# Four chained layers on one core: the attentions' exponentials go through one set of score banks, with bfloat16 row maxima

## What is computed

```python
scores = jnp.einsum('bshd,bmhd->bhsm', qh, kh) / jnp.sqrt(hd)   # layer 3: masked columns get -1e9
probs  = jax.nn.softmax(scores, axis=-1)                        # over the 77 context rows
out    = jnp.einsum('bhsm,bmhd->bshd', probs, vh)               # then a 256x256 projection and the residual
```

## Time and profile before

| | |
|---|---|
| median of 3 runs | 912.06 us |
| the profiled execution | 911.81 us |
| its span, first to last instruction | 909.6 us |
| PE, DVE and ACT busy | 92%, 57%, 49% of the span |
| mean granted TensorE clock | 0.977 of full speed |

### The profile page before, as it was taken

The page is one execution under the profiler, slowest core; times in us unless marked ns, Lnnn a source line. Parts: engine busy times, 40 slices in busy tenths (PEclk is TensorE's granted clock), DMA queues, the critical chain, the costliest instruction groups (busy, mean ns, idle before and its releaser), DMA issues.

```text
span 909.6 us, 10241 instructions
## 1 busy us (share of the span) xinstructions
PE 836.3 (92%) x4229; PEld 382.9 (42%) x4232; DVE 517.2 (57%) x714; ACT 449.9 (49%) x662; POOL 48.5 (5%) x41
## 2 busy tenths in 40 slices
PE   5998999989899999987998998999888989888987
PEld 2544444444344445452324244234355434544342
DVE  3368999843431032167636035479679495994442
ACT  3586322554434225252442723667865468752634
POOL 1000000020000000012200000000021000210000
PEclk9999999999999999988899999999989999999999
DMA  7000000011000000030000000000000000000011
GB/s 291 1 1 1 0 0 1 15 79 47 2 0 1 0 1 0 1 138 0 1 1 1 1 0 1 1 0 0 1 1 1 1 0 1 1 1 1 1 47 47
DMA packets 3004, 15.60 MB, mean 17 GB/s; under 512 B 656, under 2 KB 912, under 8 KB 2320
## 3 DMA queue, kind: packets, MB, share of 16 engines
q1 hardware_dynamic: 2816, 12.88, 3.8%
q0 software_dynamic: 144, 2.10, 0.5%
HBM read 12.87 MB, written 2.10 MB: 16 GB/s over the span
## 4 chain that ended last, share of the span: by engine, by line
PE 72%; ACT 15%; DVE 10%; DMA 2%; issue 1%; SPq 0%; POOL 0%; DVEq 0%; ACTq 0%
PE ps L421 70%; DVE VB L669 3%; ACT AR L653 3%; DMA WA<-in_m 2%; ACT AR L1923 2%; ACT AR L1913 1%; DVE AR L2236 1%; ACT AR L1607 1%; DVE AR L685 1%; ACT AR L1889 1%; ACT AR L658 1%; ACT AR L656 1%; DVE AR L511 1%; ACT AR L1906 1%; ACT AR L1919 1%
## 5 line engine op out<-in xcount | busy, mean ns | idle before, releaser
L421 PE MATMUL ps<-AR,WA 128*128 128x512 f32 (+2 forms) x716 | 310.9, 599 | 8.1 <-DVE AR L2469 3.6
L421 PEld LDWEIGHTS ps<-AR,WA 128*128 128x128 f32 (+2 forms) x716 | 131.7, 190 | 174.9 <-issue 159.1
L421 PE MATMUL ps<-AR 128*64 128x128 f32 (+5 forms) x680 | 100.6, 424 | 8.7 <-ACT AR L1923 2.0
L421 PE MATMUL ps<-AR,CN 128*128 128x512 f32 (+3 forms) x304 | 102.8, 599 | 4.8 <-DVE AR L514 1.9
L421 PEld LDWEIGHTS ps<-AR 128*64 128x64 f32 (+4 forms) x680 | 53.3, 166 | 48.2 <-issue 22.4
L685 DVE TENSOR_TENSOR AR<-ps,AR 128x512 f32<-128x512 f32 x24 | 16.6, 692 | 99.4 <-ACT AR L658 99.4
L653 ACT ACTIVATE AR<-ps 77x2048 f32<-77x2048 f32 x24 | 43.9, 1868 | 42.3 <-PE ps L421 31.1
L669 DVE TENSOR_REDUCE VB<-ps 128x16 f32<-128x1232 f32 x32 | 44.9, 1438 | 29.4 <-PE ps L421 28.6
L421 PEld LDWEIGHTS ps<-AR,CN 128*128 128x128 f32 (+2 forms) x304 | 35.2, 157 | 52.2 <-issue 35.0
L421 PE MATMUL ps<-KB,WA 128*128 128x512 f32 (+1 forms) x120 | 53.0, 609 | 0.9 <-ACT AR L1906 0.9
L2366 DVE SCALAR_TENSOR_TENSOR AR<-AR,VC 128x512 f32<-128x512 f32 x72 | 50.6, 748 | 5.4 <-ACT AR L1847 4.4
(11 more groups left out here) (334 smaller groups left out, 1124.7 us busy)
## 6 DMA issues: line engine op xcount, KB each, us to landing
WA<-in_m SPq DMA_DIRECT2D x1, 2856.0 KB, 9.6
WA<-in_m SPq DMA_DIRECT2D x1, 2560.0 KB, 15.8
X<-in_xT POOLq DMA_DIRECT2D x1, 2048.0 KB, 9.5
WA<-in_m SPq DMA_DIRECT2D x1, 2048.0 KB, 8.4
out<-X SPq DMA_DIRECT2D x4, 512.0 KB, 3.1
WB<-in_m SPq DMA_DIRECT2D x1, 1024.0 KB, 4.8
AR<-in_rows SPq DMA_DIRECT2D x1, 640.0 KB, 10.2
WA<-in_m SPq DMA_DIRECT2D x1, 512.0 KB, 16.6
```

What stands on the lines that cost most here:

```text
L421: return nc.tensor.matmul(out, lhsT, rhs, start=first, stop=last)
```

## The change

- `attn_pe`, `attn_act`: one set of score banks, 0 to 3, for both batch entries. The items (g, b, k) are worked in turn: the scores of item n+1 wait for the exponential of item n, and the weighing of item n is issued behind the scores of item n+1. The group's outputs get banks of their own, `out_bank`: banks 4 to 7 (pairs = 2), or 4 and 5 alone (pairs = 1, in "a2" j = 1 and "a3" j = 0, where banks 6 and 7 take the neighbours' means). With pairs = 1 the weighing of a (g, b) waits for `att_ctx` of the one before it.
- The ones are weighed first and have a semaphore of their own, `att_den`; the inverse of an item is issued on ACT behind the exponential of the item after it.
- `maxima_dve`: the maxima go to fp32 `MXF`; two small DVE operations split them into two bfloat16 parts in `MXP`. They are turned by a bfloat16 product with an identity, and added by a bfloat16 selecting column (`SEL16`) with `MXT` in bfloat16.
- Two places hold fp32 products of constants whose result nothing reads: one of 512 and one of 128 columns in the head, behind the turning of entry 0, and two of 512 columns behind the scores of the first item.
- The neighbours' pieces are hung on other items; the second mean of squares of "a3" j = 0 comes behind the whole attention (`second_squares`). In "a0" j = 1 the wait for `norm_xn` moves behind the first exponential.
- The constants grow from 944 to 1010 columns. Some semaphores are shared.

```diff
-        MXP = [VB[:, b * 1024:b * 1024 + T].rearrange("p (s n) -> p s n", s=SUB) for b in range(B)]
-        MXT = [VB[:, b * 1024 + T:b * 1024 + 2 * T] for b in range(B)]
+        MXP = [VB[:, b * 1024:b * 1024 + T // 2].bitcast(BF16).rearrange("p (s n) -> p s n", s=SUB) for b in range(B)]
+        MXT = [VB[:, b * 1024 + T // 2:b * 1024 + T].bitcast(BF16) for b in range(B)]
+        MXF = [VB[:, b * 1024 + T:b * 1024 + T + SUB * 16].rearrange("p (s r n) -> p s r n", s=SUB, r=4) for b in range(B)]
...
-                pe.wait_ge(*after("att_mx", nset(p, j, len(sets) - 1, b)))
+                pe.wait_ge(*after("att_mp", nunit(p, j, b)))
                 for s in range(SUB):
-                    last = nc.tensor.transpose(bank(b, 0)[:, s * P:(s + 1) * P], MXP[b][:, s, :], cn("ident"))
+                    last = mm(bank(b, 0)[:, s * P:(s + 1) * P], MXP[b][:, s, :], ID16)
                 last.then_inc(sem("att_mt"), 1)
-
-        def attn_pe(pe, p, j, masked=False, qs=QS, ready=None, meanwhile=None, begun=False):
-            sets = key_sets(p)
+                if b == 0:
+                    mm(bank(0, 2), cn("ident"), CN[:, 0:T])
+                    mm(bank(0, 2)[:, 0:P], cn("ident"), CN[:, 0:P])
...
+        def out_bank(b, pairs, to):
+
+            return ps[:, 4 + 2 * (b % pairs) + to, :]
...
+            def scores(n):
+                g, b, k = items[n]
+                if g == 0 and k == 0:
+                    pe.wait_ge(*after("att_mc", nunit(p, j, b)))
+                if n:
+                    pe.wait_ge(*after("att_ex", nitem(p, j, *items[n - 1])))
+                i = sets.index((g, k))
+                for r in range(4):
+                    row = slice(32 * r, 32 * r + 32)
+                    mm(bank(0, r)[0:M, :], KF[row, k, g, b, :], qs[b][row, g, :], True, False)
+                for r in range(4):
+                    row = slice(32 * r, 32 * r + 32)
+                    last = mm(bank(0, r)[0:M, :], SEL16[row, i:i + 1].broadcast_to([32, M]), MXT[b][row, :], False, True)
+                last.then_inc(sem("att_p2"), 1)
+
+            def weighed(n):
+                g, b, k = items[n]
+                pe.wait_ge(*after("att_ex", nitem(p, j, g, b, k)))
+                if (g, b, k) == (0, 0, 0):
+                    pe.wait_ge(*after("att_mc", nunit(p, j, B - 1)))
+                elif k == 0 and g * B + b >= pairs:
+                    pe.wait_ge(*after("att_ctx", CHUNKS[p] + nk(j, DC * B, g * B + b - pairs)))
+                for to in (1, 0):
+                    for r in range(4):
+                        head = slice(g * P + 32 * r, g * P + 32 * r + 32)
+                        lhsT = ONEP[p][k] if to else VS[:, k, b, head]
+                        last = mm(out_bank(b, pairs, to)[32 * r:32 * r + 32, :], lhsT, PTX[b][:, k, r, :], k == 0, k == PARTS[p] - 1)
+                    if k == PARTS[p] - 1:
+                        last.then_inc(sem("att_den" if to else "att_pv"), 1)
+
+            scores(0)
+            pe.wait_ge(*after("att_mp", nunit(p, j, B - 1)))
+            for k in range(2):
+                mm(bank(1, 2 + k), cn("ident"), CN[:, 0:T])
+            for n, (g, b, k) in enumerate(items):
+                if n + 1 < len(items):
+                    scores(n + 1)
+                weighed(n)
+                if meanwhile:
+                    meanwhile(g, b, k)
...
+            def inverse(g, b):
+                act.wait_ge(*after("att_den", nchunk(p, j, g, b)))
+                nc.scalar.activation(RTB[b], out_bank(b, pairs, 1), ACT.Ln).then_inc(sem("att_ln"), 1)
+                act.wait_ge(*after("att_ln", nchunk(p, j, g, b)))
+                nc.scalar.activation(RTB[b], RTB[b], ACT.Exp, scale=-1.0).then_inc(sem("att_r"), 1)
+                if meanwhile:
+                    meanwhile(g, b)
+
+            items = attn_items(p)
+            for n, (g, b, k) in enumerate(items):
+                act.wait_ge(*after("att_p2", nitem(p, j, g, b, k)))
+                nc.scalar.activation(PTX[b][:, k], ps[0:M, 0:4, :], ACT.Exp, bias=bias).then_inc(sem("att_ex"), 1)
+                if freed and n == 0:
+                    freed()
+                if k == 0 and n:
+                    inverse(*items[n - 1][:2])
+            inverse(*items[-1][:2])
...
+            for i, (g, k) in enumerate(sets):
                 for b in BS:
                     if second and (i, b) == (1, 1):
                         second()
                     dve.wait_ge(*after("att_p1", nset(p, j, i, b)))
-                    where = MXP[b].rearrange("p s (r n) -> p r s n", n=32)
+                    where = MXF[b].rearrange("p s r n -> p r s n")
                     nc.vector.tensor_reduce(where[:, :, :, i] if PARTS[p] == 1 else where[:, :, 2 * k:2 * k + 2, 2 * g:2 * g + 2],
                                             ps[:, 4 * b:4 * b + 4, 0:HALF].rearrange("p r (s m) -> p r s m", m=M), AX.X, ALU.max, negate=True).then_inc(sem("att_mx"), 1)
+                    if i == len(sets) - 1:
+                        parts = MXP[b].rearrange("p s (r n) -> p s r n", n=32)
+                        exact, upper, lower = MXF[b][:, :, :, 0:i + 1], parts[:, :, :, 0:i + 1], parts[:, :, :, 4:5 + i]
+                        dve.wait_ge(*after("att_mx", nset(p, j, i, b)))
+                        nc.vector.tensor_copy(upper, exact).then_inc(sem("att_mh"), 1)
+                        dve.wait_ge(*after("att_mh", nunit(p, j, b)))
+                        nc.vector.tensor_tensor(lower, exact, upper, ALU.subtract).then_inc(sem("att_mp"), 1)
...
+        def attn_dve(dve, p, j, meanwhile=None, then=None, begun=False, pairs=2):
             if not begun:
                 maxima_dve(dve, p, j)
             if meanwhile:
                 meanwhile()
             for g in range(DC):
-                if first and g == 0:
-                    first()
                 for b in BS:
                     dve.wait_ge(*after("att_r", nchunk(p, j, g, b)))
-                    nc.vector.tensor_tensor(ST[b][:, g, :], bank(b, 0), RTB[b], ALU.mult).then_inc(sem("att_ctx"), 1)
-                if then and g == 0:
-                    then()
+                    dve.wait_ge(*after("att_pv", nchunk(p, j, g, b)))
+                    nc.vector.tensor_tensor(ST[b][:, g, :], out_bank(b, pairs, 0), RTB[b], ALU.mult).then_inc(sem("att_ctx"), 1)
+                    if then:
+                        then(g, b)
...
+            def first_squares(g, b, k):
+                if (g, b, k) == (0, 0, 1):
+                    for u in BS:
+                        pe.wait_ge(*after("norm_sqs", NORMS["x3"] + u + 1))
+                        mm(bank(1, 2 + u), cn("mean"), SQ2[u][:, 0, :]).then_inc(sem("norm_ms"), 1)
+                elif (g, b, k) == (1, 1, 0):
                     pe.wait_ge(*after("norm_ln", NORMS["x3"] + B))
+                    for u in BS:
+                        pe.wait_ge(*after("ra_sqs", u + 1))
+                        mm(bank(1, 2 + u), cn("mean"), SQA[u][:, 0, :]).then_inc(sem("ra_ms"), 1)
 
             pe.wait_ge(*after("kv_kb", KEYS["a2"] + 4))
             pe.wait_ge(*after("oz", 3))
@@ -1334,7 +1381,7 @@
                 mm(bank(b, 0), cn("mean"), SQ2[b][:, 0, :]).then_inc(sem("norm_mean"), 1)
             queries2(1, [1])
             pe.wait_ge(*after("norm_xc", CENTRED["x3"] + B))
-            attn_pe(pe, "a2", 1, ready=first_read, meanwhile=first_squares)
+            attn_pe(pe, "a2", 1, meanwhile=first_squares, pairs=1)
...
+            def second_squares():
+                pe.wait_ge(*after("norm_xc", CENTRED["l3"] + 2 * B))
+                for u in BS:
+                    pe.wait_ge(*after("norm_sqs", NORMS["l3"] + B + u + 1))
+                    mm(bank(1, 2 + u), cn("mean"), SQL[u][:, 0, :]).then_inc(sem("norm_ms"), 1)
...
-            act.wait_ge(*after("norm_xn", NORMS["r2"] + B))
-            attn_act(act, "a0", 1, table=False)
+            attn_act(act, "a0", 1, table=False, freed=lambda: act.wait_ge(*after("norm_xn", NORMS["r2"] + B)))
...
+            def second_normed(g, b):
+                if (g, b) == (0, 0):
+                    centred3(1)
+                elif (g, b) == (0, 1):
+                    squares3()
+
+            attn_dve(dve, "a3", 0, lambda: sums3(1), second_normed, pairs=1)
```

152 lines of the change are left out of this document (55 added, 97 removed).

## The result

The changed kernel took 915.01 us (median of 11, 912.03 to 917.00), the kernel before 911.22 on the same chip (median of 11): ratio **1.0046, interval 1.0029 to 1.0063**. By the ratio it is slower by 4.2 us where +1.5 was forecast; the range held it. Medians are of all executions and ratios leave out the few that ran slow (in run 7 one of six, 1123.65 us, without which its median is 924.66). The profiled execution took 916.61 us, span 914.5, so 4.9 more span than before.

What follows compares the result with a forecast made beforehand. TensorE was taken to bound the kernel (72% of the chain), other engines counting only where it waits. Second halves -3.67, heads +5.04 and constants' transfer +0.1 made +1.5 on 911.81: 913.3 us, range 909.8 to 916.8 for 8 in 10.

Steps and rivals of the forecast that it cites:

- The item: One round of scores and exponential with one score set: 3.31 us, in "a3" 3.40, with the weighing covered.
- The heads: First reduction to first scores of the second half: small DVE operations lengthen the six heads by +5.0 us together.
- rival 2: In the heads, small DVE operations cost 0.3 us each, 7.2 instead of 5.0, total 915.5; chance 0.1.
- "a3" j = 0, the queue: Squares queued on DVE ahead of the third product delay the fourth weighing: +2.7 us, with PE waiting about 2.4.
- rival 1: In "a3" j = 0 the clock falls to 1.2 GHz for 3.4 us: +1.7, total 915.0; chance 0.25.
- Its point of decision: In "a3" j = 0, whether the clock falls depends on the wait being nearer 2.7 than 1.25 us.
- "a0" j = 0, second half: First scores of the second half to first product of the output projection: 15.13 us against 16.03, so -0.90.
- Constant products, "nothing": In the heads and behind the first scores, they lie under DVE's reduction and the first exponential: no cost.
- The sum: Second halves -3.67, heads +5.04, constants' transfer +0.1: +1.5 us in all.
- the overlap: With smaller products, it gains in four attentions' second halves what the heads and "a3" j = 0's DVE queue give back.

Runs made afterwards that it cites:

- run 7: The changed kernel with its maxima in float32 again, one score set and constant products kept: 926.12 us, ratio 1.0183.
- run 1: The changed kernel with VectorE's squares in "a3" j = 0 spread over three of its gaps: 913.65 us, ratio 1.0041.
- run 3: The changed kernel with GpSimd's scaling of the feed-forward weight held until both entries' maxima of the first attention are split: 915.87 us, ratio 1.0066.
- one_set_mended: The changed kernel with squares spread, constant products in two more waits, GpSimd's scaling held, entry 1's split reordered in five heads: 909.91 us, ratio 1.0005.
- runs 1 to 3: Run 1, run 3 and, between them, the changed kernel with two constant products in TensorE's 2.27 us wait in "a3" j = 0: 913.38 us, ratio 1.0049.
- no_constants: The changed kernel without the constant products in the two waits of each attention's head: 938.12 us, ratio 1.0325.
- parts_alone: The kernel before with the two-part bfloat16 maxima alone, two score sets, no constant products: 914.18 us, ratio 1.0030.
- runs 10 and 11: `parts_mended` (run 10) and `one_set_mended` (run 11): ratios 0.9940 and 1.0005.
- run 6: `parts_alone` with constant products in each head's first wait and entry 1's split moved behind the copy of entry 0: 916.15 us, ratio 1.0068.
- parts_mended: `parts_alone` with first-wait constant products, one more ahead of the test, "a0" j = 1's first exponentials earlier, GpSimd's scaling held: 904.83 us, ratio 0.9940.

## Why the prediction was right or wrong

- **The item** (3.31, in "a3" 3.40): 3.28 and 3.37. The selecting product, taken as 0.40, takes 0.39 to 0.42. The four second halves whose clock held came within 0.14 of the sum. Right.
- **The heads**: five of six came to +4.39, where +4.2 was summed. Small operations of 0.18 and 0.2 were right, rival 2 was not. The sixth, "a0" j = 0, was +2.29 and not +0.84: the term lacks GpSimd's work beside it. I had sized the two operations from rows in which GpSimd was idle or had just begun, and not asked what ran there in the new place; without the collision it is +0.63.
- **"a3" j = 0, the queue**: squares 2.35 and 1.29 ahead of the third product, a wait of 2.27 (2.4 forecast). Right, in mechanism and size.
- **"a3" j = 0, the clock**: this was rival 1 at 0.25, and it is what happened, at twice its price: half clock from 857.5 to 864.3, 6.8 us with PE busy, costs 3.2 and not 1.7 (21.74 at full clock, 24.97 here). That rival 1's total of 915.0 is the measured 915.01 is luck: it had this fall at half its price, and neither "a0" j = 0 nor what fell away elsewhere. Its point of decision, the length of the one wait, between 1.25 and 2.7, does not hold: with 1.51 the clock fell as well (run 1), and in "a0" j = 0 it fell behind waits of 0.68 and 1.25 (run 3), where the kernel before has the same 1.25 and keeps it.
- **"a0" j = 0, second half**: 15.13 forecast, 16.38 measured, and 15.14 in `one_set_mended` at full clock. The term was sized rightly and the clock left out.
- **Constant products, "nothing"**: as work they cost nothing, but the sum went by rows at full clock, and full clock is what they buy; without them the change is 1.0325. The step that put them at nothing was right only since they were there. I named what hid them and not what they kept up.
- **The sum**, -3.67 + 5.04 + 0.1: in the profiles the second halves +1.06, the heads +6.69, the rest -2.85. The terms that missed are the two of "a0" j = 0 (+1.45, +1.25) and the clock of "a3" j = 0 (+3.5), 6.2 together; the rest of the span, which the sum put at nothing and where this pair of profiles has 14 us less of half clock, gave back 2.9. The forecast was 913.3 against 911.81 before, ratio 1.0016, where 1.0046 came out: inside the range of 909.8 to 916.8, but outside the forecast's own 911.5 to 914.8 and inside rival 1's 914 to 916.5. That the falls of "a0" j = 0 and "a3" j = 0 carry the difference is not shown: mending one or the other alone (runs 1 to 3) left the ratio at 1.004 to 1.007.
- What the prediction credited to "the overlap" was no gain. With equal maxima and clock the second halves of the one set are 5.7 us longer; the forecast compared one set with bfloat16 to two sets with float32 and never asked for two sets with bfloat16.

## What to carry to other kernels

When a change has two parts, work out each part alone against the kernel before: here one part gains about 4 us at full clock and the other loses about 6, and with the earlier exponential's 1 the sum looked like no change. When a change makes TensorE's products shorter or its chain more serial, cost the clock as a term of its own, and look for it in the granted clock of each stretch; here the constant products in the waits ahead were worth 25 us and the change cost 4. Judge such a mend by the time of the runs, for a fall that is gone in one profile need not be gone in the others. And ask of a small operation on the critical chain what every other engine does at that moment.

## What the runs showed of the hardware

- TensorE's clock fell without any long wait. In `no_constants` it was at half rate for 10.2 to 13.7 us in each attention, behind waits of 1.4 to 2.3 us, and in `parts_alone` it fell in all six, behind waits of 1.4 to 2.4. It stayed up in all six second halves of the kernel before, whose waits there are 0.7 to 1.3 and whose turning and selecting products are float32, and with bfloat16 products where constant products stood in the waits (all six in runs 10 and 11, "a2" and "a3" in run 6). Shorter waits and longer products come together in the kernel before, so which of the two keeps the clock there is not shown. What exactly decides stays open: neither the one wait's length (1.25 and 1.82 without a fall, 1.25 with one) nor the kind of product (in run 7 it fell in "a3" j = 0 with float32) alone sorts the runs.
- Two operations of VectorE on 32 elements a partition took 0.96 and 1.06 us instead of 0.18 and 0.19 beside GpSimd operations of 2.85 us on SBUF, but only where GpSimd's first had begun while VectorE's earlier subtraction ran. The Trainium skill (SBUF — State Buffer, Who interferes with whom) has VectorE and GpSimd share a pair of ports under an exclusive lock: where both want it, whichever issues first has it for the whole instruction and the other is blocked. The trace agrees for the cast, which in all three profiles ended 0.04 behind GpSimd's first operation. It differs otherwise: the subtraction ended at 190.52, 1.7 us before GpSimd's second operation did, and in four profiles neither was blocked, though the same instructions ran side by side. Why is open.
- A constant product queued behind the reading of the test's flag and the branch on it started after 0.89 us in which nothing else held TensorE (`parts_mended`, the product at 190.20; 0.98 in `one_set_mended`) and held up the scores behind it by 0.7. Whether the reading or the branch takes that time is not shown. Filling a wait is free only where the queue gets to the filler in time.
